# Squared norms of keys and queries: ScalarE's accumulator in place of a VectorE reduction

## The reference

```python
qkv_c = sum((xp[:, j:j + Tq, :] * conv_w[:, j] for j in range(KC)))   # causal convolution, 4 taps
q = _l2norm(qkv_c[..., :QD].reshape(Bq, Tq, NK, DK))                  # x / sqrt(sum(x*x))
k = _l2norm(qkv_c[..., QD:2 * QD].reshape(Bq, Tq, NK, DK))
...
def step(S, inp):                                                     # the delta rule, token by token
    q_t, k_t, v_t, b_t, d_t = inp
    Sk = jnp.einsum('bhi,bhipj->bhpj', k_t, S)
    dv = b_t[..., None] * (v_t - Sk)
    S = S * d_t[:, :, None, :, None] + jnp.einsum('bhi,bhpj->bhipj', k_t, dv)
    return (S, jnp.einsum('bhi,bhipj->bhpj', q_t, S))
out = out * rms * norm_w                                              # rms over the 128 of a value head
y = jnp.einsum('btd,cd->btc', out.reshape(Bq, Tq, VD) * jax.nn.silu(z), W_out)
```

## Time and profile before

| | |
|---|---|
| median of 3 runs | 1954.21 us (1953.55 to 1955.62) |
| the profiled execution's own time | 1953.7 us |
| its span | 1952.0 us |
| mean granted TensorE clock | 0.988 of full speed |
| PE, ACT, DVE, POOL busy | 97%, 88%, 92%, 74% of the span |

### The profile page before, as it was taken

One profiled execution on the slowest core, in us unless ns is written; L12 is line 12 of the kernel. 1 busy time (PEld: TensorE's weight loads), 2 busy tenths in 40 slices (PEclk: granted clock), 3 DMA queues, 4 the chain that ended last, 5 costly groups with the idle time before them and its releaser, 6 DMA issues.

```text
span 1952.0 us, 62169 instructions
## 1 busy us (share of the span) xinstructions
PE 1892.3 (97%) x23622; PEld 1564.1 (80%) x23622; DVE 1794.6 (92%) x2907; ACT 1724.4 (88%) x3527; POOL 1444.3 (74%) x1083
## 2 busy tenths in 40 slices
PE   7699999999999999999999999999999999997999
PEld 6478888888888888888888888888888888876788
DVE  7789999999999999999999999999999999985987
ACT  7589999999999999999999999999999999985332
POOL 5467887887787878787878787787878887774452
PEclk9799999999999999999999999999999999998999
DMA  3000000000000000000000000000000000012000
GB/s 121 13 16 11 3 25 3 25 2 25 3 25 3 25 2 11 16 3 25 3 25 3 25 3 24 3 25 3 6 22 3 24 3 3 24 38 83 26 15 22
DMA packets 18008, 35.92 MB, mean 18 GB/s; under 512 B 5804, under 2 KB 14508, under 8 KB 15412
## 3 DMA queue, kind: packets, MB, share of 16 engines
q1 hardware_dynamic: 17716, 31.95, 4.8%
HBM read 29.30 MB, written 2.64 MB: 16 GB/s over the span
## 4 chain that ended last, share of the span: by engine, by line
POOL 45%; issue 23%; DVE 12%; PE 10%; ACT 9%; POOLq 1%; DVEq 0%; DMA 0%; ACTq 0%; SPq 0%
PE bank L686 9%; POOL a_lo L535 7%; POOL invT L572 7%; POOL go L556 6%; POOL b_le L510 6%; POOL osc L546 5%; POOL q L488 4%; DVE ae L1943 4%; POOL w L481 3%; POOL rn L500 3%; ACT kn L1427 3%; DVE n2m L1924 3%; DVE y_acc L2038 2%; POOL solv L580 2%; ACT inv L1479 2%
## 5 line engine op out<-in xcount | busy, mean ns | idle before, releaser
L1904 DVE SCALAR_TENSOR_TENSOR cc<-bank,wc,cc 128x510 f32<-128x510 f32 (+2 forms) x768 | 551.7, 739 | 7.8 <-ACT cc L1394 0.8
L686 PE MATMUL bank<-h,w 128*128 128x512 f16 (+1 forms) x1920 | 424.5, 362 | 2.7 <-issue 2.5
L686 PEld LDWEIGHTS bank<-h,w 128*128 128x128 f16 x1920 | 173.5, 99 | 134.8 <-issue 8.0
L1484 ACT ACTIVATE invT<-bank 128x512 f16<-128x512 f32 x384 | 245.0, 638 | 6.1 <-PE bank L686 4.6
L1972 DVE TENSOR_TENSOR yl<-bank,mask 128x512 f16<-128x512 f32 x320 | 218.2, 682 | 4.4 <-PE bank L686 4.4
L1479 ACT ACTIVATE inv<-bank 128x512 f16<-128x512 f32 x320 | 207.7, 649 | 9.8 <-PE bank L686 9.8
L1394 ACT ACTIVATE cc<-bank,wc 128x512 f32<-128x512 f32 x256 | 177.7, 694 | 15.8 <-PE bank L686 14.8
L686 PE MATMUL bank<-w,h 128*128 128x256 f16 x1536 | 190.7, 275 | 0.0
L686 PE MATMUL bank<-w,goT 128*128 128x256 f16 x1536 | 188.6, 272 | 0.0
L686 PEld LDWEIGHTS bank<-inv,a 128*128 128x128 f16 x3072 | 136.7, 98 | 52.1 <-ACT inv L1479 6.3
L500 POOL TENSOR_TENSOR rn<-n2m,mhalf 128x4 f32<-128x4 f32 x64 | 64.5, 1008 | 131.7 <-DVE n2m L1917 131.7
(11 more groups left out here) (236 smaller groups left out, 5606.6 us busy)
## 6 DMA issues: line engine op xcount, KB each, us to landing
w_raw<-in_wh SPq DMA_DIRECT2D x15, 1032.0 KB, 4.8
out<-sol SPq DMA_DIRECT2D x16, 128.0 KB, 1.7
v<-in_x SPq DMA_DIRECT2D x3, 512.0 KB, 3.7
moving<-rank_store SPq DMA_DIRECT2D x64, 8.0 KB
standing<-rank_store SPq DMA_DIRECT2D x64, 8.0 KB
w_raw<-in_wgate SPq DMA_DIRECT2D x1, 1024.0 KB, 5.0
cc<-in_wup SPq DMA_DIRECT2D x1, 1024.0 KB, 4.7
pt<-gate_store SPq DMA_DIRECT2D x2, 512.0 KB, 4.2
```

The lines of the kernel that those rows point to most:

```text
L686: return mm(o_, l_, r_, start=start, stop=stop, skip_group_check=True)
L1484: A(rights(invT[:, ring(s)], l), halves(bL[1], l), ACT.Copy).then_inc(sig("xt_ready"), 1)
L1904: V.scalar_tensor_tensor(dst, src, wc[:, par(s), i, 3 - j:4 - j], dst, ALU.mult, ALU.add).then_inc(sig(f"conv{i}"), 1)
```

## The change

ScalarE's one square of 128x512 becomes four squares of 128x128, and each of them also gives the sum of its results along the row (`accum_out`), straight into its column of `n2`. VectorE's two sums for each step go. The guards wait for four increments of `sq0` or `sq1` where they waited for one of `n2`, and two waits of ScalarE on `n2` go. `sq` is still written.

```diff
                 n = N(s)
                 need(act, ("kt_ps", "qt_ps")[i], n + 1)
-                need(act, "n2", n * 2)
-                A(sq[:, i], grid(bS[0] if i and n == 0 else bB[i]), ACT.Square).then_inc(sig(f"sq{i}"), 1)
+                for t in range(TL):
+                    A(sq[:, i, t], grid(bS[0] if i and n == 0 else bB[i])[:, t], ACT.Square,
+                      accum_out=n2[:, blk(s), i, t:t + 1]).then_inc(sig(f"sq{i}"), 1)
...
                 if j == 0:
                     act.wait_ge(sig("modT_ready"), 4)
-                    act.wait_ge(sig("n2"), STEPS * 2)
...
-            def squared_norms(i, s):
-
-                n = N(s)
-                need(dve, f"sq{i}", n + 1)
-                V.tensor_reduce(n2[:, blk(s), i], sq[:, i], AXX, ALU.add).then_inc(sig("n2"), 1)
-
             def guarded_keys(s):
                 n = N(s)
-                need(dve, "n2", n * 2 + 1)
+                need(dve, "sq0", n * TL + TL)
...
             def guarded_queries(s):
                 n = N(s)
-                need(dve, "n2", n * 2 + 2)
+                need(dve, "sq1", n * TL + TL)
...
-                if s0:
-                    squared_norms(0, s0)
...
-                if s0:
-                    squared_norms(1, s0)
```

## The result

| | before | after |
|---|---|---|
| median, runs taken together | 1953.88 us (1951.21 to 1955.62) | 2020.47 us (2019.59 to 2022.47) |
| ratio, 95% interval | | 1.0342 (1.0329 to 1.0355) |
| span of the profiled execution | 1952.0 us | 2019.5 us |
| one steady step | 26.46 us | 27.54 us |

The forecast was 2010, with a range of 1966 to 2075.

A forecast was written before the change was run, and what follows sets the result against it. The prediction took PE (TensorE) to bound the kernel, busy 26.43 of 26.45 us in a steady step. It summed 1953.7 us + 54.9 (61 steps at 0.90) + 1 for pipeline filling = 2009.6, so 2010, range 1966 to 2075.

The forecast's parts named there:

- What bounds: Steady step: PE busy 26.43 of 26.45 us, so relief elsewhere gains at most 0.02 us and any PE wait lengthens it.
- VectorE's sums: Removing VectorE's 128 sums, 1.35 us in a step, shortens nothing; the time becomes idle time before existing waits.
- The small squares: On ScalarE, a 128x128 square has a pitch of 0.16 us, so four take 0.64 in place of 0.48.
- The accumulator read: Writing out each small square's sum costs ScalarE 0.095 us, taken from the tap weights' pitch.
- The cheap: Rival: ScalarE's read-out costs 0 to 0.05 us, 9 to 33 us in all, ending at 1962 to 1987; chance 0.18.
- the dear: Rival: ScalarE's read-out costs 0.19 us, 101 us in all, ending at 2056; chance 0.25, including 0.07 for the fully serial form.
- the serial sum: Rival: each read-out waits for its square and the next square waits for it, 2.94 us a step, 2134; chance 0.07.
- The cover: Normed keys are ready 0.18 us before PE turns them, so 1.08 us of added ScalarE work costs 0.90 a step.
- The pipeline's filling: The two steps in which the pipeline fills lose between 0 and 1.8 us, taken as 1.
- The places of the waits: PE would newly wait on `u1` or `invT` behind the first squares, 0.5 us, and on the normed keys, 0.4.
- The signs given for the profile after: Step 27.3 us, ACT busy over 26, DVE about 23.9, DVE idle 0.6 larger before `second_output` and the keys' low half.

The follow-up runs named there:

- e5: The kernel before, with VectorE summing only in the first four steps and later steps using the first head's norms; ratio 0.9995, step 26.45 us.
- e9: The kernel before with four unread 128x80 copies added at the end of ScalarE's round, in front of the tanh; ratio 1.0001, step 26.45 us.
- e8: The kernel before with four unread 128x80 copies added on ScalarE ahead of the output squares and normed keys; ratio 1.0187, 37 us slower.
- e6: The kernel after with VectorE's sums put back, written to a spare tile nobody reads; ratio 1.0328 against the kernel before.
- e1: The kernel before with each square cut into four of 128x128, no accumulators, VectorE's sums kept; ratio 1.0101, 20 us slower.
- e2: The kernel before with two whole squares, each with one accumulator read into a spare tile, VectorE's sums kept; ratio 1.0045, 9 us slower.
- e3: The kernel before with the change made for the keys alone, the queries keeping one square and VectorE's sum; ratio 1.0165, 32 us slower.
- e4: The kernel before with the change made for the queries alone, the keys keeping one square and VectorE's sum; ratio 1.0167, 33 us slower.
- e7: The kernel after with ScalarE's output squares moved behind the normed keys; ratio 1.0523 against the kernel before, 102 us slower.
- e11: The kernel after, keys' squares moved behind four operations, output squares behind normed keys and inverse level 4, VectorE's keys guard ahead of its output sum; ratio 1.0823.

## Why the prediction was right, and which term was off

**What bounds.** Right in what the sum uses, too strong in its reason. PE's 26.43 us of work in 26.45 was read as: relief is worth nothing, a wait is paid in full. e5 shows the first half for VectorE's sums (1.35 us less, no change), e9 that work in front of an idle place costs nothing, e8 the second half. But PE isn't full in that step. Its weight loads wait 0.16 us for VectorE's `yl` and 0.18 for its `solv` in every step; the rows are of the waits of the kernel before, over 56 steps, then of VectorE's timeline:

```profile
PEld bank L686 <- DVE solv L1984: 9.9, 56, 0.2
PEld bank L686 <- DVE yl L1972: 8.9, 56, 0.2
```

```profile
940.06 0.68 DVE L1972 TENSOR_TENSOR yl<-bank,mask 128x512 f16<-128x512 f32 x1
```

That `yl` ends at 940.74, and the level product starts 0.06 later, at 940.80. The four products ahead of it start at 940.42, 0.38 before it, where the same four take 0.22 elsewhere in the step (937.20 to 937.42): PE stands still for 0.15 us, inside its busy figure. So "nothing that frees another engine can shorten such a step by more than 0.02 us" doesn't follow from the busy time. It is shown for the sums, which stand elsewhere; no run made `yl`, `solv` or ScalarE's part ahead of them faster.

**VectorE's sums.** Right, at no worth; e5 and e6.

**The small squares.** Right: 0.16 us. The estimate from the Trainium skill's figure ("ScalarE: Activation LUTs", section "What ACT_TABLE_LOAD costs"), 0.20 us for 128 elements and 0.52 for 512, is high for these operations out of PSUM: the trace shows 0.16 and 0.48, and by 0.56 us for the split e1 would have lost 34 us over 61 steps, not 20.

**The accumulator read.** Right: an instruction of its own, 0.09 us to the next start where 0.095 was taken from the tap weights. The cheap, the dear and the serial sum fall.

**The cover.** This is the term that was mis-sized. I took 0.18 us off, the time from the end of ScalarE's normed keys to the start of TensorE's turn of them, and forecast a loss of 0.90 us in a step where 1.08 was lost. 0.18 over 61 steps is 11 us, which is what the forecast was short of. Two smaller slips nearly cancel in it: the squares add 1.04 and not 1.08, and ScalarE's operations last longer, as told below. The pipeline's filling costs 2.5 us by the third step's keys, where I took 1. The table gives PE's time between four of its own starts in a step: from the second `us,kx` products (`query_state`) to the level product behind the first squares, on to the output product (`sol,pt`), on to the turn of the keys, and from there to the next `us,kx`. Each is the distance of two starts in PE's timeline, in us.

| | to level 3 | to output | to keys | to next | sum over before |
|---|---|---|---|---|---|
| before | 4.69 | 0.95 | 4.54 | 16.28 | |
| e2, two reads | 4.75 | 0.97 | 4.54 | 16.34 | 0.14 |
| e1, split | 4.85 | 0.97 | 4.59 | 16.37 | 0.32 |
| e3, keys | 5.22 | 0.97 | 4.54 | 16.28 | 0.55 |
| e4, queries | 4.69 | 0.95 | 4.97 | 16.38 | 0.53 |
| after | 5.21 | 0.98 | 4.96 | 16.38 | 1.07 |

Three things made up the cover that wasn't there. First, at the level product nearly all of the 0.17 us between ScalarE's end (940.63) and PE's start (940.80) was not slack but the hand-over. PE waited for VectorE's `yl` there, but with `yl` sooner it could have started at most 0.03 sooner: in the kernel after PE waits for just that half, which is ready at 1002.53 + 0.68 = 1003.21, and starts at 1003.35, 0.14 later. So 0.03 was cover, and 0.52 of added work costs 0.52 there. I named this product, but did the sum with the output product behind it. Second, at the normed keys some 0.12 of the 0.18 was real (0.06 remains when PE waits: 1009.23 to 1009.29), and e4 loses 0.43 of its 0.52 there. Third, what is saved there is paid behind it. I wrote that nothing gives time back behind the keys, and so stopped adding there. But once PE has waited for the keys, its turn of them takes 0.06 us longer: from its start to the next products 1009.29 to 1009.78, where it was 946.29 to 946.73; the first of the four now has 0.16 us to the next start, and the others 0.11 as before. And ScalarE's queue is late by the whole amount and PE only by part of it, so a later hand-over takes the rest. It is the last rows of the inverse, `yl`. Before, they were ready and taken as follows, ACT first, and in the kernel after at 1010.73 + 0.59 = 1011.32 and 1011.37:

```profile
947.60 0.59 ACT L1491 ACTIVATE yl<-bank 64x512 f16<-64x512 f32 x1
...
948.27 0.40 PE L686 MATMUL bank<-invT,yl 128*128 128x64 f16 x8
```

0.08 us between the two then, 0.05 now, so 0.03 of cover. A late engine meets several hand-overs, and the tightest of them sets what is lost. The 0.10 in the column "to next" of e4 and after is the longer turn (0.06) and this wait (0.04: `w,h` to this product takes 1010.02 to 1011.37, where it took 946.96 to 948.27). It doesn't stand there in e3, where the whole delay was paid at the first.

A small part is left: the step grew by 1.08 and the start-to-start times by 1.04. While ScalarE works without a gap, the recorded duration of its operations grows; the four copies of the keys last 1.32 us against 1.23 and start 1.00 later, so their end comes 1.09 later. That agrees with the step, and in e4 (end 0.55 later, step 0.53) and e8 (0.62 and 0.59) too. Why it grows, no run here takes apart.

**The places of the waits.** Right for the normed keys. The prediction named `u1` for the first, with the level product in brackets; it is the level product, 0.53 us. On `u1` itself PE's weight loads wait 0.3 us, of which a few hundredths are lost.

**The signs given for the profile after.** The step was to be 27.3 and is 27.54; ACT busy over 26 of it, 26.59; DVE 23.9, 23.63. DVE's idle time grew in front of `second_output` from 0.30 to 0.95 us and in front of the keys' low half from 0.48 to 1.27, where some 0.6 each was named.

## What to carry to other kernels

When one engine shows next to no idle time, read another engine's worth by place: here work in front of what that engine took next was paid nearly in full (0.59 of 0.64 us in e8, 0.15 of 0.18 in e2), and the same work in front of a wait was free (e9), whatever the two busy shares say. Such an engine need not be full: look at the waits of its weight loads and at the start-to-start times too. The gap between a producer's recorded end and the consumer's start is hand-over first (here 0.14 us at the level product, 0.06 at the keys) and cover only in what exceeds it, and a delay must be followed through all the hand-overs behind it, since the tightest one charges it. Folding a reduction into the operation before it is no saving if it costs more instructions on the engine that is watched (here 0.52 us on ScalarE for each 0.68 us that VectorE didn't need back).

## What the runs showed that I had not expected

**A 128x4 clamp on VectorE that lasts up to 1.45 us.** The queries' guard, two small operands, lasts 0.88 us in the kernel before, 0.16 in the kernel after, 1.12 and 1.45 in e7 and e11, in the groups of VectorE over the steady part. In that order:

```profile
L1924 DVE TENSOR_SCALAR n2m<-n 128x4 f32<-128x4 f32 x57 | 50.2, 881 | 0.0
```

```profile
L1918 DVE TENSOR_SCALAR n2m<-n 128x4 f32<-128x4 f32 x54 | 8.9, 165 | 0.0
```

```profile
L1918 DVE TENSOR_SCALAR n2m<-n 128x4 f32<-128x4 f32 x53 | 59.6, 1124 | 0.0
```

```profile
L1917 DVE TENSOR_SCALAR n2m<-n 128x4 f32<-128x4 f32 x52 | 75.6, 1454 | 0.0
```

GpSimd's output gate is running beside it, and in e11 it shows until when:

```profile
1027.32 2.37 POOL L528 TENSOR_TENSOR osq<-o,zg 128x1024 f32<-128x1024 f32 x1 [1.93 <-DVE oss L2007]
```

It ends at 1029.69, and the guard that started at 1028.25 ends at 1029.71. The same holds in the kernel before (gate to 949.66, guard 948.81 to 949.69) and in e7 (1031.70, 1030.60 to 1031.72). The Trainium skill has this in "SBUF — State Buffer", section "Who interferes with whom": a VectorE operation in a two-port mode and GpSimd lock each other out for a whole instruction. The trace agrees in the times; that it is this port and nothing else, no run here isolates. In the kernel after the guard starts at 1011.93, 0.12 us before the gate ends (1012.05), and is over at 1012.09. So its 3% in the chain of the page before went with the change, and shortened nothing.

**A second chain close behind.** Output squares, VectorE's sum of them, GpSimd's gate, the guard behind it, `decayed_keys` and `z_gate` form a chain on which PE hardly waits in the kernel before, and on which it does when ScalarE's output squares move back. VectorE waits 1.6 us for them in e7 and 2.7 in e11. Of the 0.55 us by which e7's step is longer than the kernel after's, 0.26 lie behind `yl`, 0.15 of them at the wait for `zg`; the rest is the inverse's level behind the keys. In e11 the part behind the keys' low half is about 0.6. How much of e11's loss is this chain's, and how much comes from its other edits, no run takes apart.
